# Transposing a residual straight into the accumulation banks, and finishing one unit as rows on GpSimd, in a four-sequence transformer kernel

## What is computed

```python
h = gelu(einsum('bsh,bhk->bsk', y, W_down[role]) + b_down)      # 512 -> 256
u = einsum('bsk,bkh->bsh', h, W_up[role]) + b_up                # 256 -> 512
z = y + u
z = (z - mean(z)) * rsqrt(var(z) + eps)
y = z * gamma[role] + beta[role]
...
# three such layers, one after the other, on sequences of shape (4, 512, 512)
```

## Time and profile before

| | |
|---|---|
| three runs | 1179.77, 1181.37, 1182.26 us, median 1181.37 |
| profiled execution | 1180.58 us |
| its span, first to last instruction | 1178.7 us |
| mean granted TensorE clock | 0.998 |
| busy: PE, weight loads, DVE, ACT, POOL | 1167.0, 965.8, 761.7, 531.5, 162.3 us |
| adapter stage on PE | from 1010.49 us to the end |

### The profile page before, as it was taken

How to read it: one execution, slowest core, us unless ns; L and a number is a source line. 1 busy time by engine, 2 the same in 40 slices (tenths; PEclk the granted TensorE clock), 3 DMA queues, 4 the chain that set the end, 5 groups by cost and what they waited for, 6 DMA issues and landing times.

```text
span 1178.7 us, 15577 instructions
## 1 busy us (share of the span) xinstructions
PE 1167.0 (99%) x5276; PEld 965.8 (82%) x5276; DVE 761.7 (65%) x1352; ACT 531.5 (45%) x965; POOL 162.3 (14%) x146
## 2 busy tenths in 40 slices
PE   9999999999999999999999999999999999999997
PEld 8878888878888788888888888888888888788886
DVE  6345386776767865656567676785555646777786
ACT  5434354564544534343435535433131313347887
POOL 1332130000000000000000000000000000349981
PEclk9999999999999999999999999999999999999999
DMA  5754543536644726263699789756777679946645
GB/s 209 265 208 166 181 176 119 179 136 231 211 159 176 259 100 245 104 234 124 233 406 313 234 295 309 212 188 193 230 192 231 192 230 298 342 144 218 224 166 197
DMA packets 113045, 251.25 MB, mean 213 GB/s; under 512 B 13364, under 2 KB 13364, under 8 KB 109638
## 3 DMA queue, kind: packets, MB, share of 16 engines
q1 hardware_dynamic: 112822, 249.99, 62.6%
q10 hardware_dynamic: 144, 0.26, 0.1%
HBM read 154.78 MB, written 95.43 MB: 212 GB/s over the span
## 4 chain that ended last, share of the span: by engine, by line
PE 89%; DVE 5%; DMA 3%; ACT 2%; issue 1%; POOL 1%; SPq 0%; DVEq 0%; ACTq 0%
PE psum L749 85%; DMA prep<-wdu_dram 2%; PE psum L1022 2%; POOL prep L1965 1%; DMA wd<-wdu_split 1%; DVE c_op L1631 1%; PE psum L803 1%; ACT prep L1062 0%; ACT res L1366 0%; PE psum L798 0%; PE psum L814 0%; DVE dg L1679 0%; DVE ring L1521 0%; DVE res L1703 0%; PE psum L783 0%
## 5 line engine op out<-in xcount | busy, mean ns | idle before, releaser
L749 PE MATMUL psum<-a_op,ring 128*128 128x512 f32 x1344 | 316.5, 389 | 0.3 <-DVE w_t L1563 0.3
L749 PEld LDWEIGHTS psum<-a_op,ring 128*128 128x128 f32 x1344 | 252.1, 188 | 53.2 <-DVE w_t L1563 0.8
L749 PE MATMUL psum<-g_hl,w_hl 128*128 128x512 f32 x1152 | 263.6, 389 | 0.4 <-DVE w_hl L1582 0.4
L749 PEld LDWEIGHTS psum<-g_hl,w_hl 128*128 128x128 f32 x1152 | 216.1, 188 | 46.0 <-DVE w_hl L1582 0.8
L749 PE MATMUL psum<-c_op,ring 128*128 128x512 f32 x672 | 163.3, 390 | 0.4 <-DVE c_op L1631 0.3
L749 PEld LDWEIGHTS psum<-c_op,ring 128*128 128x128 f32 x672 | 125.8, 188 | 27.8 <-DVE c_op L1631 1.8
L1178 ACT ACTIVATE g<-g,sm 128x512 f32<-128x512 f32 x96 | 69.5, 724 | 137.4 <-DVE g L1569 66.7
L1589 DVE TENSOR_TENSOR g_hl<-g,g_hl 128x512 fp32r<-128x512 f32 x96 | 66.1, 689 | 52.0 <-ACT g_hl L1201 51.1
L1158 ACT CAST ring<-asum 128x256 fp32r<-128x256 f32 x96 | 38.5, 404 | 104.3 <-PE psum L749 76.1
L1971 POOL MEMSET acc_u<- 128x1024 f32 x1 | 1.0, 955 | 592.4 <-DVE w_hl L1582 592.4
L1201 ACT CAST g_hl<-g 128x512 fp32r<-128x512 f32 x96 | 58.5, 618 | 53.2 <-PE psum L749 53.2
(11 more groups left out here) (156 smaller groups left out, 1589.4 us busy)
## 6 DMA issues: line engine op xcount, KB each, us to landing
up_operands<-ring SPq DMA_DIRECT2D x168, 256.0 KB, 2.6
ring<-up_operands SPq DMA_DIRECT2D x168, 256.0 KB, 3.0
wdu_split<-prep SPq DMA_DIRECT2D x36, 512.0 KB, 2.9
down_operands<-stage SPq DMA_DIRECT2D x56, 256.0 KB, 4.9
ring<-down_operands SPq DMA_DIRECT2D x56, 256.0 KB, 3.0
rawp<-up_w_dram SPq DMA_DIRECT2D x24, 512.0 KB, 4.9
wraw<-dn_w_dram SPq DMA_DIRECT2D x48, 256.0 KB, 3.9
wu<-wdu_split SPq DMA_DIRECT2D x12, 1024.0 KB, 5.4
```

Of the source, the lines that this page charges most:

```text
L749: ins = nc.tensor.matmul(ps, lw(el), rw(er), start=first and i == 0, stop=last and i == 2, skip_group_check=skip)
```

## The change

It has two parts. **First layer's residual.** y0 is no longer turned into rows by a round trip over DVE. `y0_transposed(b)` puts the 16 transposes into `UP[0..3]` as the opening of the accumulation (start flag on the first of each bank), and the up product is accumulated on top. It is called at the head of `t_up_mm(b)`, for all four sequences. `z_stats` then adds the up bias rows instead of the residual. The 16 DVE additions of `y0_rows` and two semaphores go. Since `UP[2]` and `UP[3]` now are written right behind transpose(b-2), `y0_transposed` waits for `t_yf` of these banks when b is 2 or 3. On SP the down weights of unit 1 and the up weights of unit 0 move ahead of the loads of y0.

**Unit 8.** It is not transposed on PE and not scaled by ACT. POOL finishes it as rows, 8 more operations, with loaded rows of gamma and beta, and it is stored as rows.

```diff
-            for u in (8, 9):
-                sp.wait_ge(t_yf, (u + 1) * DT)
-                sp.dma_start(out[u % B], res[:, u % B, :, :]).then_inc(s_out, 16)
+            sp.wait_ge(t_res, 9 * DT)
+            sp.dma_start(out[0], res[:, 0, :, :]).then_inc(s_out, 16)
+            sp.wait_ge(t_yf, turned(10))
+            sp.dma_start(out[1], res[:, 1, :, :]).then_inc(s_out, 16)
...
-            def y0_to_rows(b, tiles=range(DT)):
+            def y0_transposed(b):
 
                 if b < 2:
                     pe.wait_ge(s_y0in[b], 16)
                 else:
                     pe.wait_ge(y0_done, DT * b)
-                for i in tiles:
+                for i in range(DT):
                     if b == 0:
                         pe.wait_ge(e_done, e_count(NCH - 1, 1, i - 2) if i >= 2 else e_count(NCH - 1, 4, i))
-                    if b == 1:
-                        pe.wait_ge(t_res_done, i + 1)
-                    if b > 1:
-                        pe.wait_ge(t_z, (b - 2) * DT + i + 1)
+                    else:
+                        pe.wait_ge(t_z, (b - 1) * DT + i + 1)
+                    if b >= 2 and i >= 2:
+                        pe.wait_ge(t_yf, (b - 2) * DT + i - 1)
                     for d in range(DT):
-                        ins = nc.tensor.transpose(UP[i][:, d * P:(d + 1) * P],
-                                                  res[:, b, d, i * P:(i + 1) * P], ident[:, :])
-                    ins.then_inc(t_rows_full, 1)
+                        nc.tensor.matmul(UP[i][:, d * P:(d + 1) * P], res[:, b, d, i * P:(i + 1) * P], ident[:, :],
+                                         start=d == 0, stop=False, is_transpose=True, skip_group_check=True)
...
             def t_up_mm(u, b):
+                if u < B:
+                    y0_transposed(b)
...
-                if 3 <= s:
+                if 3 <= s and s != 11:
                     t_transpose(s - 3, (s - 3) % B)
...
-                        nc.vector.tensor_tensor(z[u % 3][:, i, :], UP[i], res[:, u % B, i, :], ALU.add).then_inc(t_z, 1)
+                        rest = bup0[:, u, :] if u < B else res[:, u % B, i, :]
+                        nc.vector.tensor_tensor(z[u % 3][:, i, :], UP[i], rest, ALU.add).then_inc(t_z, 1)
...
             for s in range(14):
-                if 3 <= s < 11:
+                if 3 <= s < 12:
                     rows_scaled(s - 3, 0)
                     rows_scaled(s - 3, 1)
                     rows_shifted(s - 3, 0)
                 if 2 <= s:
                     rstd_of(s - 2)
```

More of the change, by code:

```diff
@@ L416, in build, with turned @@
         LAST_COLS, LAST_ROWS = (0, 1), (2, 3)
+        def turned(u):
+            return DT * (u - (u > 8))
         last_cols = res[:, 3, 0:2, :].rearrange("p a s -> p (a s)")
@@ L673, in unit_rows @@
                 sp.dma_start(bc[b % 2][:, 0, :], gb_all[bass.ds(row, 1), 0].to_broadcast([P, V])).then_inc(t_bc[b % 2], 16)
-                sp.dma_start(bc[b % 2][:, 1, :], beta_bup[bass.ds(row, 1)].to_broadcast([P, V])).then_inc(t_bc[b % 2], 16)
+                if u < 8:
+                    sp.dma_start(bc[b % 2][:, 1, :], beta_bup[bass.ds(row, 1)].to_broadcast([P, V])).then_inc(t_bc[b % 2], 16)
+                else:
+                    sp.dma_start(bc[b % 2][:, 1, :], gb_all[bass.ds(row, 1), 1].to_broadcast([P, V])).then_inc(t_bc[b % 2], 16)
             for i in range(PSLOT):
@@ L703, in _ @@
                     unit_down_part(0, WD_AT.index(at_))
+            for k in range(len(YT_AT) - 4, 4):
+                split_rows(1, k)
+            unit_down(1)
             sp.wait_ge(s_spill, 16 * 4)
@@ L706, in _ @@
             sp.dma_start(res[:, 0, :, :], y0_dram[:, 0]).then_inc(s_y0in[0], 16)
-            for k in range(len(YT_AT) - 4, 4):
-                split_rows(1, k)
+            unit_up(0)
             sp.wait_ge(aop_used, dop_at(NCH - 1, 11) + 1)
@@ L721, in _ @@
                     unit_up(u)
-                if 4 <= u < 10:
+                if 4 <= u < 11:
                     unit_rows(u - 2, (u - 2) // B, (u - 2) % B)
@@ L983, in t_down_mm @@
                     ins.then_inc(t_down, 1)
-                    if m == 0 and u in (2, 3):
-                        y0_to_rows(u, (DT - 1,))
             def t_up_mm(u, b):
+                if u < B:
+                    y0_transposed(b)
                 pe.wait_ge(t_wu[u % 2], 16 * (u // 2 + 1))
                 for i in range(DT):
-                    if u < 3:
-                        pe.wait_ge(t_res_done, (u + 1) * DT + i + 1)
-                    else:
+                    if u >= B:
                         pe.wait_ge(t_z, (u - 1) * DT + i + 1)
-                    if 2 <= u < 11 and i >= 2:
+                    if B <= u < 10 and i >= 2:
                         pe.wait_ge(t_yf, (u - 2) * DT + i - 1)
@@ L999, in t_up_mm @@
                         ins = mm3(UP[i], lambda e: h_hl[b % 2][:, e, k, i * P:(i + 1) * P],
-                                  lambda e: wu[b % 2][:, e, k, :], k == 0, k == MT - 1)
+                                  lambda e: wu[b % 2][:, e, k, :], u >= B and k == 0, k == MT - 1, skip=u < B)
                     ins.then_inc(t_up, 1)
@@ L1035, in _ @@
                     t_up_mm(s - 1, (s - 1) % B)
-                if 1 <= s < 3:
-                    y0_to_rows(s + 1, range(DT - 1))
         @block.scalar
@@ L1362, in y_scale @@
                 for d in tiles:
-                    act.wait_ge(t_tr, u * DT + d + 1)
+                    act.wait_ge(t_tr, turned(u) + d + 1)
                     n = 2 * P
@@ L1375, in _ @@
                     h_hi(11)
-                if 11 <= s < 13:
-                    y_scale(s - 3)
+                if s == 12:
+                    y_scale(9)
                 if s < 11:
@@ L1814, in _ @@
                     down_add(ci, 1)
-            def y0_rows(b):
-                dve.wait_ge(t_bup0, 16 * B)
-                if b >= 2:
-                    dve.wait_ge(t_y0lo, (b - 1) * DT)
-                dve.wait_ge(t_rows_full, (b + 1) * DT)
-                for i in range(DT):
-                    nc.vector.tensor_tensor(res[:, b, i, :], UP[i], bup0[:, b, :], ALU.add).then_inc(t_res_done, 1)
             def factors(u, k, n):
@@ L1836, in z_stats @@
             def z_stats(u, between=None):
+                if u == 0:
+                    dve.wait_ge(t_bup0, 16 * B)
                 for i in range(DT + 2):
@@ L2070 @@
     y = np.ascontiguousarray(got.transpose(0, 3, 2, 1)).reshape(B, S, V)
+    y[0] = got[0].transpose(1, 0, 2).reshape(S, V)
     y[3, :2 * P] = got[3, :, :2].reshape(P, DT, 2 * P).transpose(2, 1, 0).reshape(2 * P, V)
```

28 lines of the change are left out of this document (7 added, 21 removed).

## The result

The changed kernel took 1183.1 us in the median of 20 runs (1180.65 to 1186.61), the kernel before 1180.3 us in 20 (1179.53 to 1182.26). The ratio is 1.0027, 95% interval 1.0020 to 1.0033: 0.27% slower, where 0.22% faster was forecast, and 2.3 us above the upper end of the stated range. The scatter (highest less lowest run) has doubled too, from 2.7 to 6.0 us. The profiled execution took 1181.98 us with a span of 1179.9; it is one of the faster ones.

A forecast was written before the change was run, and what follows sets the result against it. PE, busy for 1167.0 of 1178.7 us, was taken as the bound. 1.3 (y0 transposes) + 1.78 (unit 8) - 0.5 (tail) = 2.6 us gained, set against 1181.0: 1178.4 us, range 1176.6 to 1180.8.

The forecast's parts named there:

- the first part: The y0 transposes, from the end of the MLP to up(2): 2.14 - 0.45 - 0.4 = 1.3 us gained.
- Both are covered: Start of the stage: unit 1's weights and second y0 land before they are needed; otherwise the old 1.4 us comes back.
- the two DMA waits: PE's waits for unit 1's weights and for y0's second load, about 1.4 us together, which the new order would remove.
- Rival 3: The loads don't help: PE idles elsewhere for the 1.4 us; gain 1.2, 1179.8 us; chance 0.05.
- the tail: End of the kernel: transpose(10) starts late behind ACT and the last store with it; 0.5 us lost, ends nothing and 2.2.
- The base of the forecast: The time the gain was set against: 1181.0 us, the mean of all four executions of the kernel before.
- the low parts: DVE's two operations for unit 11, ahead of unit 10's statistics: 0.85 us each in the median beside POOL, 1.74 at most.
- Down(0): First down product of the stage: starts at 1010.9 after idling for DVE's addition, 0.45 us lost, ends 0.36 and 0.96.
- the wait for the banks: At sequences 2 and 3, y0 transposes wait for DVE's reading of UP[2] and UP[3]: 0.2 us twice, 0.4 lost.
- Unit 8's removal on PE: Second part: PE loses 1.66 us of transposes and up(10) no longer follows transposes, 0.12: 1.78 us gained.
- rival 4: POOL decides the tail: unit 8's rows delay the variance of unit 10; 4.9 us slower, 1185.9 us; chance 0.04.
- rival 5: The clock falls after 32 transposes in a row, 5.45 us more per block at two places; 1189.3 us; chance 0.02.

The follow-up runs named there:

- Down2_first: The changed kernel with unit 2's down weights issued ahead of y0 of sequence 1, unit 1's up weights and the first four row loads: 1178.14 us, ratio 0.9984.
- pool_held: The changed kernel with GpSimd held until unit 11's low parts are done, and the variance of unit 10 ahead of its last two row operations: 1181.74 us, ratio 1.0019.
- mended_y0_first: Changed kernel with unit 2's weights issued early, GpSimd held twice in the tail, first y0 transposes ahead of down(0), y0 loaded as before the change: 1178.46 us, 0.9986.

## Why the prediction was wrong

**The direction was wrong by one sentence.** The step that failed is in the first part: "Both are covered". I followed the loads that SP issues earlier (unit 1's weights, y0) and asked when each is needed in the new order. For these two it was true: unit 1's weights had landed by about 1014 for a product near 1016.4, y0 of sequence 1 by 1021.5 for 1037.4. I did not ask it of the next load in the queue, unit 2's down weights, which no line of the diff moves. They landed at 1033.1 for a product at 1033.14, and the y0 part asks for that product 4.0 us earlier. That stretch was bound by its loads, and only the two DMA waits that the change cures were visible as waits. Down2_first shows it by the one edit: 1.0027 to 0.9984. What the runs show in place of full cover is an idle stretch ahead of down(2) of 2.55, 3.15 and 4.19 us in the three profiles with these loads, as the weights took 15.0, 15.6 and 16.6 us to land. Rival 3 had the right kind of place ("PE idles elsewhere") and the wrong argument, "10 us and more of cover at each".

**The size follows from two more terms.** The median lies 5.4 us from the forecast's gain (2.6 faster forecast, 2.8 slower measured). Down2_first takes back about 5.0: the wait, 2.55 to 4.2 us, and in some executions the clock's fall behind it, 1.4 us. The rest is the tail. The base of the forecast, 1181.0, was 0.7 us above the median of the 20 runs, which is not what failed.

**The tail was mis-sized.** I took 0.5 us given back with 0 to 2.2 as ends; it was 1.24 (13.46 against 12.22). The mechanism was right, the low parts held by POOL, but they took 2.38 us where the forecast had 1.7 from the median. Missed was that the factors of unit 9 are held as well (1.25 in place of 0.16), and they stand ahead of the low parts on DVE. The Trainium skill ("SBUF — State Buffer", section "SBUF: two separate sides") says that a DVE instruction with two SBUF inputs and a GpSimd instruction that reads SBUF exclude each other for the whole instruction. The runs agree: the factors' 1.25 us are the length of the row operation beside them (1.30), and pool_held takes them away. The prediction had set a loss of 1.5 us beside that rule and taken 0.5; the 1.24 is near the former.

**What held.** Down(0) at 1010.91 for 1010.9. Transpose(0) and the y0 transposes behind it until up(2): 3.55 us (1050.11 to 1053.66), 3.52 forecast, so the wait for the banks was 0.2, though no row names it. Unit 8's removal on PE: down(11) to transpose(9) is 10.88 us against 12.68, 1.80 for 1.78. POOL had slack (1.56 us), so rival 4 did not occur; POOL cost time by what it held up on DVE, not by being late itself. The y0 part without the wait: 1.5 for 1.3. And 32 transposes in a row did not lower the clock, so rival 5 is out in its form; the clock did fall, but behind idling, and a fall cost 1.4 us, not the 5.45 that rival 5 put on it. With the wait removed (down2_first), the whole change came to 1.8 us faster in the medians against the 2.6 of the forecast; the tail's 0.74 more than forecast is about the difference.

The Trainium skill ("TensorE: Matmul & The Clock Gate", section "Part 4: PE-mode transpose") says that transposes don't count as PE work for the clock in the same way as matmuls. Down2_first, with the clock at 1.00 over both stretches of 32, shows no cost of that where matmuls stand on both sides, and mended_y0_first's transposes at 0.50 came after 2.2 us of idling.

## What to carry to other kernels

When an edit brings a point of the bound engine forward, list every load that is due behind that point, with its landing time in the old trace against its new due time, the unmoved ones above all: a load that lands just in time shows no wait and has no slack. In a queue as full as this one, the order by due time is what counts, and an earlier issue of one load can be a later landing of the next. Work given to GpSimd costs also what it holds up on DVE, down to the smallest instruction, and its own late store.

## What the runs showed that I had not expected

The same 1 MB load landed in 15.0 to 16.6, 10.0 to 11.2 or 5.3 us by its place in one queue, and 1 MB of row loads (one row copied to 128 partitions) ahead of it cost 3.8 to 6.6 us where 2 MB of ordinary loads cost 4.7 to 5.9.

The granted clock fell to 0.50 for about 3 us behind idle stretches of 4.2 us twice and behind one of 2.2 us, and stayed at 1.00 behind 2.55 and 3.15. The length alone doesn't decide; what else does stays open.

A DVE instruction on 128x4 numbers took 1.25 us beside a GpSimd row operation, 0.16 without.
